# A 48-column clear behind every gather on GpSimd, in a four-stage convolution kernel

## What is computed

```python
om = _conv3x3(x, w_om, b_om)                  # offsets and a mask for each pixel and tap
py = base_y[None] + dy;  px = base_x[None] + dx
y0 = jnp.floor(py);      x0 = jnp.floor(px)
...
sampled = gather_corner(y0, x0, (1 - fy) * (1 - fx)) + ...   # four corners
sampled = sampled * mask[:, None]
out = jnp.einsum('bckhw,ock->bohw', sampled, w.reshape(CO, C, K2))
```

## Time and profile before

| | us |
|---|---|
| median of 3 runs | 1706.59 |
| lowest and highest | 1701.79, 1708.61 |
| span of the profiled execution | 2212.2 |
| POOL busy in it | 1208.5 (55%) |
| PE busy | 1480.2 (67%) |
| DVE busy | 981.2 (44%) |
| ACT busy | 547.5 (25%) |

### The profile page before, as it was taken

One profiled execution on the slowest core, in us unless ns is written; L12 is line 12 of the kernel. 1 busy time (PEld: TensorE's weight loads), 2 busy tenths in 40 slices (PEclk: granted clock), 3 DMA queues, 4 the chain that ended last, 5 costly groups with the idle time before them and its releaser, 6 DMA issues.

```text
span 2212.2 us, 14137 instructions
## 1 busy us (share of the span) xinstructions
PE 1480.2 (67%) x4202; PEld 653.9 (30%) x4202; DVE 981.2 (44%) x1645; ACT 547.5 (25%) x874; POOL 1208.5 (55%) x1418
## 2 busy tenths in 40 slices
PE   7636651899645865957847765867847743665797
PEld 6432221343312322322313322322312311222245
DVE  3423342444422347842523247842431393323585
ACT  1111110233211231232322231231221302222446
POOL 8645455456465546566546546566546475565230
PEclk9867875899767887978967877978967985778899
DMA  6211221231212112321212112321212111211100
GB/s 198 56 52 49 55 55 51 69 91 51 60 46 75 47 37 60 82 58 43 68 33 77 51 37 59 82 59 43 59 40 56 29 50 40 64 42 49 31 8 13
DMA packets 111883, 123.08 MB, mean 56 GB/s; under 512 B 50880, under 2 KB 88896, under 8 KB 111424
## 3 DMA queue, kind: packets, MB, share of 16 engines
q0 software_dynamic: 36864, 75.57, 12.6%
q1 hardware_dynamic: 73888, 43.14, 7.6%
q10 hardware_dynamic: 1056, 3.47, 0.4%
HBM read 99.79 MB, written 9.01 MB: 49 GB/s over the span
## 4 chain that ended last, share of the span: by engine, by line
PE 33%; another core or an unknown queue 26%; DVE 17%; issue 15%; ACT 7%; DMA 1%; SPq 1%; DVEq 0%; ACTq 0%
PE bank L1960 6%; PE bank L1973 5%; DVE rb L1733 4%; PE bank L1875 4%; PE bank L1885 3%; PE bank L1867 3%; DVE gt L1617 3%; PE bank L1910 3%; PE bank L1943 2%; PE bank L1996 2%; DVE he L1515 1%; PE bank L1982 1%; DVE gt L1619 1%; DVE bst L1440 1%
## 5 line engine op out<-in xcount | busy, mean ns | idle before, releaser
L1137 POOL DMA_INDIRECT gt<-corner_table,idx x1152 | 1135.0, 985 | 877.1 <-DVE sm L1625 493.7
L1973 PE MATMUL bank<-yg,wts 128*128 128x512 f32 x512 | 252.2, 636 | 56.5 <-issue 30.9
L1960 PE MATMUL bank<-u,wk 128*128 128x512 f32 x512 | 254.0, 642 | 14.2 <-ACT yg L1298 4.0
L1659 DVE SCALAR_TENSOR_TENSOR tg<-tg,ae 128x512 f32<-128x512 f32 x64 | 44.4, 694 | 403.6 <-ACT ae L1310 342.0
L1875 PE MATMUL bank<-xg,w_sb 128*128 128x512 f32 (+1 forms) x288 | 156.1, 626 | 68.4 <-issue 38.9
L1515 DVE SCALAR_TENSOR_TENSOR he<-he,bank 128x512 f32<-128x512 f32 (+1 forms) x144 | 89.9, 626 | 206.0 <-remote 83.0
L1885 PE MATMUL bank<-he,w_sb 128*128 128x512 f32 (+1 forms) x288 | 150.1, 606 | 35.3 <-DVE he L1515 26.8
L1617 DVE TENSOR_TENSOR gt<-gt,bank 128x1152 f32<-128x1152 f32 x128 | 172.5, 1347 | 1.1
L1867 PE MATMUL bank<-xp,w_sb 128*128 128x512 f32 (+1 forms) x288 | 151.5, 610 | 20.3 <-ACT he L1212 13.6
L1212 ACT ACTIVATE he<-bank 128x512 f32<-128x512 f32 (+1 forms) x144 | 79.1, 549 | 307.6 <-PE bank L1867 157.3
L1733 DVE SCALAR_TENSOR_TENSOR rb<-xp,par,rb 128x1024 f32<-128x1024 f32 x124 | 155.1, 1292 | 0.0
(11 more groups left out here) (249 smaller groups left out, 1557.3 us busy)
## 6 DMA issues: line engine op xcount, KB each, us to landing
gt<-corner_table,idx POOLq DMA_INDIRECT x1152
tb<-gate_of_token SPq DMA_DIRECT2D x56, 256.0 KB
u<-sqb SPq DMA_DIRECT2D x48, 128.0 KB
corner_table<-tb SPq DMA_DIRECT2D x36, 128.0 KB, 2.9
w_sb<-w ACTq DMA_DIRECT2D x2, 1024.0 KB, 6.8
xp<-xg SPq DMA_DIRECT2D x56, 32.0 KB
X<-x SPq DMA_DIRECT2D x1, 1536.0 KB, 10.9
out<-X SPq DMA_DIRECT2D x6, 256.0 KB
```

The lines of the kernel that those rows point to most:

```text
L1137: pool.indirect_dma_start(gt[:, t % GRING, k].rearrange("p a c -> p (a c)"), None, corners, bass.IndirectOffsetOnAxis(ap=idx[s % 2][:, j, ...
L1960: op = mm(psum[b][:, :], wk[:, t, d], u4[:, g, at:at + HALF], start=t == 0, stop=t == JJ - 1 and n > 0)
L1973: op = mm(psum[B2.bank(*name)][:, :], w_glu[:, k, col + d * P:col + (d + 1) * P], yg[:, c % 2, k], start=k == 0, stop=k == NB2 - 1)
```

## The change

A buffer of 48 columns is added, and behind every gather POOL clears it and waits for the end of that clear. Nothing reads the buffer. The lines behind the first edit move by one, those behind the second by two.

```diff
         rowoff = sb("rowoff", [P, 1])
+        spacer = sb("spacer", [P, 48])
         tb = sb("tb", [P, TRING, 2, GI, 2 * C])
...
                         bass.IndirectOffsetOnAxis(ap=idx[s % 2][:, j, g * KK + k:g * KK + k + 1], axis=0),
                     ).then_inc(gathered[t % GRING], 16)
+                    ch.then(pool.memset(spacer[:, :], 0.0))
 
             run(pool, dict(sample=sample))
             pool.wait_ge(S["smp_ready"], FROM + NS * NT * GI)
```

## The result

The changed kernel takes 1883.15 us (median of 4 runs, 1878.47 to 1888.89), the kernel before 1705.49 us (4 runs, 1701.79 to 1708.61). The ratio is 1.1043, with a 95% interval of 1.1015 to 1.1071: 177.7 us slower, 0.154 us for each of the 1152 gathers. The forecast was 1960 us, 254 us slower, and its range began at 1790.

A forecast was written before the change was run, and what follows sets the result against it. POOL's gathers were taken as the bound from 75 us on. The gap of 0.305 us becomes 0.115 + 0.14 + 0.27 = 0.525, so 1152 x 0.22 = 253 us on 1706.6 gives 1960 us; range 1790 to 2180.

The forecast's parts named there:

- The bound: POOL bounds the timed run from 75 us on, needing 1491 us for 1152 gathers, 1.29 us each.
- the ring waits: Rival, chance 0.07: POOL's waits for DVE, 493.7 us in the profile, hide the clears; 1707 us.
- The clear: The clear of 48 columns on POOL behind each gather takes 0.14 us.
- The restart behind the wait: From the clear's end to the next gather's start on POOL: 0.27 us.
- From the gather's end to the clear: On POOL, 0.115 us pass between a gather's end and its clear, from a gap of 0.305 us.
- the low end: Nothing between gather's end and clear: 0.105 us more a gather, 121 us in all, 1828 us.
- its own sign: Wrong in size if spacing grows by other than 0.22 us while the time follows it at 1152 times that.
- Contention: Clears could be slowed under L3's taps as gathers are: nothing in the sum, 44 us within the range.
- The spacing rival: Chance 0.05: the next gather gets ready during the clear, costing 0.076 us each, 88 us in all; 1794 us.
- PE did not take over: Rival, chance 0.04: PE, granted a clock of 0.5 throughout, bounds the stretch with gathers; 2275 us.
- The clear was not left out of the program: Rival, chance 0.02: the clear, which nobody reads, is left out of the program; 1707 us.
- What would show it: Profile after: clear 0.14 us, starting 0.1 us after its gather; next gather 0.27 us later; gathers 1.47 us apart.

The follow-up runs named there:

- The second profile: The kernel before, run and profiled once more with no edit: 1704.55 us against 1704.08, ratio 1.0004.
- two clears: The changed kernel with a second clear of 48 columns behind each gather, both waited for: 2124.96 us, ratio 1.2477.
- five columns: The changed kernel with clears of 5 columns in place of 48, each waited for: 1849.53 us, ratio 1.085.
- the unwaited clear: The changed kernel with clears of 5 other columns each, only the ninth of a tile waited for: 1727.52 us, ratio 1.0126.
- the wait alone: The kernel before with a POOL wait for each gather's own step and no clear: 1716.69 us, ratio 1.0078.
- the changed kernel without taps: The changed kernel without DVE's taps from the third on in the first three groups of L3: 1828.31 us, ratio 1.0719.
- one clear a tile: The changed kernel with the clear and its wait only behind the ninth gather of each tile: 1724.02 us, ratio 1.0121.

## Why the prediction was right, and where its sum was off

**The bound** was right: POOL from 75 us on, with the ring waits of the profiled execution left out. The second profile gives 1151.3 + 348.8 = 1500.1 us for gathers and gaps, where the prediction used 1491. The time of the changed kernel follows POOL's spacing up (two clears, five columns). What the prediction did not see is how close behind POOL the next bound is, 58.5 us.

**The clear**: 0.14 us forecast, 0.152 at the median, 0.157 in the mean, 181.2 us in all against 161.

**The restart behind the wait**: 0.27 us forecast, 0.271 measured. Its row was a gather released by DVE; a release by POOL itself is as quick.

**From the gather's end to the clear** is the step that failed. The prediction had no row, split the gap of 0.305 into 0.115 behind the gather and 0.19 ahead of the next one, and took the 0.115. Measured is 0.001 us: the clear starts as the gather ends, which was the low end. That is 0.114 × 1152 = 131 us too much. The split came from small POOL operations, and a gather is not one of them. One of its two values is misread besides: in the listing no wait stands between L1035 and L1036, so the 0.06 us are not those of an operation that waits. The whole gap is the run-up of the next gather, as the unwaited clear shows. The spacing is therefore not 0.22 us longer but 0.122, 141 us in all, near the low end's 121. By its own sign the prediction is thus wrong in its size, though the time lies in its range.

**Contention** was put at nothing, with 44 us in the range, and it was looked for at the clear. The taps do not hold up a clear: all 85 that start while one runs take 152 or 153 ns. This agrees with the Trainium skill (SBUF — State Buffer, "Who interferes with whom"), by which a two-input DVE instruction does not contend with a GpSimd instruction that only writes. Other DVE operations do hold it up. 19 of the 1152 clears take over 200 ns, and every one of them starts while DVE runs an operation with one full-size input, a TENSOR_SCALAR or a CAST; 40 clears in all start under such an operation. The longest:

```profile
129.56 0.80 DVE L1536 TENSOR_SCALAR xpad<-X,mv,rs 32x1024 f32<-32x1024 f32 x1
129.73 0.70 POOL L1142 MEMSET spacer<- 128x48 f32 x1
```

All 19 together lose 6 us. The larger part of the contention is with the gathers, which take 37.6 us more than before, 30 of it by the taps. The same section of the Trainium skill says that where a DVE operation seems to stall a DMA, it was one whose descriptors GpSimd makes. The gathers of 1.97 to 2.00 us under taps are DMAs issued by GpSimd, which agrees; which part of their work waits, no run shows. The clear costs there by changing the gathers' step, not by itself.

**Two terms that no step had**: 12 pauses, 12 × (1.56 − 0.27) = 15.5 us, and −18.3 us of ring waits, which are real in a small way. Together: 141 + 15.5 + 37.6 − 18.3 = 175.8 us of the 179.1 in the rows. Set against the forecast's 253 us: 131 too much in one step, 20 too little for the clear (181.2 against 161), 53 in terms that had been left out, and 18 that the ring gave back, 253 − 131 + 20 + 53 − 18 = 177. That the time came as near to the forecast as it did is in part luck: what one step had too much was partly made good by terms that the sum had put at nothing or too low.

**The rivals.** The ring waits hid 18 us and not 253. The spacing rival (0.076 us, 1794 us) is near the unwaited clear, which costs less still, since it lies within the run-up; it is the wait that rules the rival out, as the prediction had it. PE did not take over: its granted clock in the stretch goes from 0.88 to 0.85, its busy time from 1199.1 to 1235.5 us of 1700.2. The clear was not left out of the program.

**What would show it**: the clears, the 0.27 us and the median gather (950 ns against 947) are as foreseen; the clear 0.1 us behind the gather and the spacing of 1.47 us are not. That the ring waits shrink was right (2.8 us). That the profiled span would grow by less than the timed runs could not be judged on the first profile; on the second one it grows by 181.5 us and the runs by 177.7, so it does not.

## What to carry to other kernels

A gap between two instructions of a queue may be the run-up of the second, as the 0.305 us here: work that nobody waits for then fits into it nearly free, and the same work with a wait behind it costs its own length and the whole run-up again, less the gap that it replaces. So ask of each added instruction who waits for it, before asking how long it takes. And where a profiled span is far above the timed median, find out which rows make up the difference, and profile again before taking a wait in it for real.

## What had not been expected of the hardware

**A pause every 90 gathers.** In the changed kernel the gather at 236.36 waits 1.56 us for nothing that the trace names:

```profile
234.65 0.15 POOL L1142 MEMSET spacer<- 128x48 f32 x1
236.36 0.96 POOL L1138 DMA_INDIRECT gt<-corner_table,idx  x1 [1.56 <-issue]
```

This happens 12 times, ahead of gathers 113, 203, 293 and so on to 1103 (counted from 0), exactly 90 apart: the "issue: 18.7, 12" of the rows above (12 × 1.56 = 18.7). It is at the same numbers in all kernels with a wait behind every gather (five columns, two clears, the wait alone, and the changed kernel without taps), and in none of the others (before, the wait at the ninth, one clear a tile). In the kernel with the wait alone 12 × (1.56 − 0.30) = 15.1 us is about what it loses (1716.69 − 1702.79 = 13.9). Whether POOL does the same thing in the other kernels hidden behind gathers, and what it is, stays open.

**Engines in step.** DVE's taps and POOL's gathers fall into a common period of 1.25 us in the kernel before, at some 0.05 us a tap and nothing a gather, and a tenth of a microsecond more on POOL turns that into one gather to two taps. A small cost on one engine can so be followed by one of another kind, which no sum of durations has.
